# Dealing the copies of the turned attention heads to ScalarE and VectorE in another order, in a transformer-like kernel bound by TensorE

## What is computed

```python
q = einsum('btc,hdc->bhtd', x, Wq); k = einsum('btc,hdc->bhtd', x, Wk)      # 16 heads of 64
w, sel = top_k(einsum('btc,hec->bthe', x, Ws), 2)                          # 2 of 8 experts
v = einsum('bthe,bted->bhtd', mix(sigmoid(w), sel), einsum('btc,edc->bted', x, Wv))
probs = softmax(einsum('bhid,bhjd->bhij', q * scale, k))
attn = einsum('bhij,bhjd->bihd', probs, v)
out = einsum('bthe,bthd,efd->btf', mask_of_top_2(x, Wd), attn, Wo)
x = x + 0.5 * out
```

## Time and profile before

| what | us |
|---|---|
| median of 3 runs (lowest, highest) | 2604.54 (2603.84, 2607.11) |
| the profiled execution, its own time | 2602.62 |
| its span in the trace | 2600.8 |
| busy: PE, DVE, ACT, POOL | 2476.2, 2108.7, 1924.7, 1139.0 |
| busy as a share of the span | 95%, 81%, 74%, 44% |
| clock granted to TensorE, mean | 0.994 of full speed |

### The profile page before, as it was taken

The page is one execution under the profiler, slowest core; times in us unless marked ns, Lnnn a source line. Parts: engine busy times, 40 slices in busy tenths (PEclk is TensorE's granted clock), DMA queues, the critical chain, the costliest instruction groups (busy, mean ns, idle before and its releaser), DMA issues.

```text
span 2600.8 us, 111020 instructions
## 1 busy us (share of the span) xinstructions
PE 2476.2 (95%) x45824; PEld 2319.8 (89%) x45824; DVE 2108.7 (81%) x3498; ACT 1924.7 (74%) x6117; POOL 1139.0 (44%) x1126
## 2 busy tenths in 40 slices
PE   4999999999999999999999999999999999999997
PEld 3899999999899999999999899999999999999987
DVE  4788888888888888888888888888888888888874
ACT  3777777777777777777777777777777777777774
POOL 2344544434434444445345344444444453444431
PEclk8999999999999999999999999999999999999999
DMA  4555555565555655555655555556556556556553
GB/s 128 146 144 153 141 154 144 151 152 155 146 154 149 160 145 153 156 146 152 156 149 152 149 155 150 152 148 162 145 153 156 148 150 158 146 146 159 153 148 97
DMA packets 519346, 387.53 MB, mean 149 GB/s; under 512 B 214080, under 2 KB 436160, under 8 KB 510656
## 3 DMA queue, kind: packets, MB, share of 16 engines
q1 hardware_dynamic: 518416, 379.60, 54.6%
q10 hardware_dynamic: 432, 0.85, 0.1%
HBM read 191.64 MB, written 188.74 MB: 146 GB/s over the span
## 4 chain that ended last, share of the span: by engine, by line
PE 68%; ACT 15%; DVE 8%; issue 7%; POOL 1%; DMA 1%; SPq 0%; ACTq 0%; DVEq 0%; POOLq 0%
PE psT L451 14%; PE psS L408 14%; ACT PB L761 9%; PE psS L490 5%; PE psT L490 5%; PE psT L468 5%; PE psT L421 5%; PE psT L463 5%; PE psT L469 4%; PE psT L470 4%; DVE NMAX L639 4%; PE psT L435 4%; ACT PT L857 3%; ACT QK L770 1%; DVE QK L696 1%
## 5 line engine op out<-in xcount | busy, mean ns | idle before, releaser
L761 ACT ACTIVATE PB<-psS,NMAX 128x256 f32<-128x256 f32 x2048 | 951.4, 489 | 533.4 <-DVE NMAX L639 533.4
L639 DVE TENSOR_REDUCE NMAX<-psS 128x4 f32<-128x1024 f32 x512 | 602.1, 1217 | 79.8 <-PE psS L408 78.8
L451 PE MATMUL psT<-V,PT 128*64 128x64 f32 x16384 | 543.1, 224 | 18.1 <-issue 17.5
L451 PEld LDWEIGHTS psT<-V,PT 128*64 128x64 f32 x16384 | 503.3, 138 | 47.8 <-issue 22.7
L696 DVE TENSOR_TENSOR QK<-psT,QK 128x512 fp32r<-128x512 f32 x512 | 340.9, 688 | 177.0 <-ACT QK L770 174.9
L408 PE MATMUL psS<-QK 64*128 64x256 f32 x6144 | 434.9, 286 | 50.7 <-ACT PT L857 40.4
L408 PEld LDWEIGHTS psS<-QK 64*128 64x128 f32 x6144 | 389.8, 186 | 103.1 <-issue 100.6
L761 ACT ACTIVATION_READ_ACCUMULATOR PB<-psS,NMAX 128x1 f32 x2048 | 454.5, 222 | 0.0
L875 POOL TENSOR_TENSOR BT<-MT,diagv 128x1024 f32<-128x1024 f32 x128 | 307.8, 2405 | 115.3 <-DMA MT<-MIXd 115.3
L770 ACT ACTIVATE QK<-psT 128x512 fp32r<-128x512 f32 x512 | 295.6, 618 | 64.5 <-PE psT L470 49.5
L857 ACT ACTIVATE PT<-psS 128x512 f32<-128x512 f32 x512 | 286.4, 635 | 2.1 <-PE psS L490 1.9
(11 more groups left out here) (119 smaller groups left out, 4572.9 us busy)
## 6 DMA issues: line engine op xcount, KB each, us to landing
Vd<-VM SPq DMA_DIRECT2D x128, 512.0 KB, 3.7
V<-Vd SPq DMA_DIRECT2D x128, 512.0 KB, 5.3
AOd<-AO SPq DMA_DIRECT2D x256, 256.0 KB, 3.6
PJd<-PJ SPq DMA_DIRECT2D x64, 512.0 KB, 2.6
PR<-PJd SPq DMA_DIRECT2D x64, 512.0 KB, 4.1
MIXd<-MIX SPq DMA_DIRECT2D x64, 128.0 KB, 2.5
MT<-MIXd SPq DMA_DIRECT2D x64, 128.0 KB, 4.4
MASKd<-MASKR SPq DMA_DIRECT2D x64, 128.0 KB, 3.3
```

The costliest lines, as they stand in the source:

```text
L451: last = eng.matmul(M[64 * u:64 * u + 64, (t * NT + it) * DH:(t * NT + it + 1) * DH], PT[:, t, jt, cols], V[:, pm % 2, 4 * r + t, jt, :], ...
L639: eng.tensor_reduce(NMAX[:, ab, :, :], psS[:, ab, :, :, :], AX_X, ALU.max, negate=True).then_inc(s_max)
L761: eng.activation(PB[:, ab, j, it, :], psS[:, ab, j, it, :], ACT.Exp, bias=NMAX[:, ab, j, it:it + 1], accum_out=SUM[:, p % 2, it, 4 * r + t ...
```

## The change

DVE takes the copy of head 1 in place of head 3; ACT takes the copy of head 3 in place of head 1. DVE's copy stands ahead of L600 and L604 in quarters 0 and 2 (L600 moves down to just before L604) and where L740 was, at the end, in quarters 1 and 3. ACT's copy of head 0 stands directly behind the last exponentials in quarters 0 and 3, ahead of L828, L834, L846 and L852; in quarters 1 and 2 it stays where it was. Each engine keeps its number of copies.

```diff
2244.36 1.70 PE L408 MATMUL psS<-QK 64*128 64x256 f32 x24 vector_program
+            def copy_second(n):
+                wait_turned(eng, n, 1)
+                wait_full(eng, "product", n - 1)
+                eng.tensor_copy(PT[:, 1].rearrange("p n t -> p (n t)"), turned(n, 1)).then_inc(was_copied(n, 1))
+
             for n in QUARTERS:
...
                         eng.tensor_tensor(QK[:, 1, ab], bank("qk", m).rearrange("p (k t) -> p k t", k=2), QK[:, 0, ab].bitcast(F32), ALU.subtract).then_inc(freed("qk", m))
-                if r == 2 and runs(q):
-                    equal(1, GM[:, :, :], at + 7)
-                if r == 0 and runs(q):
-                    equal(0, GS[:, :, :], at + 1)
                 if r == 1 and runs(q):
...
                     eng.tensor_tensor(xs, bank("attn_w", p - 4)[:, 0:NT * C], xs, ALU.add).then_inc(freed("attn_w", p - 4))
+                if r in (0, 2) and works(n):
+                    copy_second(n)
                 if r == 0 and runs(q):
+                    equal(0, GS[:, :, :], at + 1)
                     weigh(at + 2)
                 if r == 2 and runs(q):
+                    equal(1, GM[:, :, :], at + 7)
                     weigh(at + 8)
...
-                if works(n):
-                    for t in (3,):
-                        wait_turned(eng, n, t)
-                        wait_full(eng, "product", n - 1)
-                        eng.tensor_copy(PT[:, t].rearrange("p n t -> p (n t)"), turned(n, t)).then_inc(was_copied(n, t))
+                if r in (1, 3) and works(n):
+                    copy_second(n)
2244.36 1.70 PE L408 MATMUL psS<-QK 64*128 64x256 f32 x24 scalar_program
+            def copy_turned(n, t):
+                wait_turned(eng, n, t)
+                wait_full(eng, "product", n - 1)
+                eng.activation(PT[:, t].rearrange("p n t -> p (n t)"), turned(n, t), ACT.Copy).then_inc(was_copied(n, t))
...
                 if r in (0, 3):
                     if works(n):
                         exponentials(n, 1, (0,))
                     if works(n + 1):
                         rounded(n)
                     if works(n):
                         exponentials(n, 1, (1,))
+                        copy_turned(n, 0)
...
                 if works(n):
-                    for t in (0, 1, 2):
-                        wait_turned(eng, n, t)
-                        wait_full(eng, "product", n - 1)
-                        eng.activation(PT[:, t].rearrange("p n t -> p (n t)"), turned(n, t), ACT.Copy).then_inc(was_copied(n, t))
+                    if r in (1, 2):
+                        copy_turned(n, 0)
+                    copy_turned(n, 2)
+                    copy_turned(n, 3)
```

## The result

The changed kernel takes 2744.65 us (median of 4 runs, 2735.25 to 2753.71), the kernel before 2605.82 us beside it: 1.0531 times as long, 95% interval 1.0490 to 1.0571. The forecast was 2725 (2640 to 2760), slower. The profiled execution took 2748.70 us with a span of 2746.9 us, so 146.1 us of span are to be accounted for.

A forecast was written before the change was run, and what follows sets the result against it. TensorE, busy 95%, was taken as the bound. To 2602.6 us came -40 + 51 + 15 + 13.5 + 9 = +48.5 and 72 for the port, 2723; with 1.9 us up to the runs' median, 2725 (2640 to 2760).

The forecast's parts named there:

- The gain of 40 us: Quarters 0 and 3: the scores no longer wait for ACT's copies of the turned heads, at most 40 us less.
- Quarter 1, the place of the copy behind L703: A1 and B1: the scores wait for DVE's copy behind the held L703, +1.0 and +0.6 us each, 51 us.
- Quarter 2: DVE's copy behind the second L696 ends after the scores' present start, +0.23 us in 64 quarters, 15 us.
- The bank waits: Turns wait for banks that ACT frees later: B0 +0.52 us each, 13.5 us; C0 and C3 together 9 us.
- The second layer: The port DVE and POOL share: DVE operations held in B0, A0, C0 and D0, 18 + 9 + 36 + 9 = 72 us.
- only the first layer: Rival: POOL doesn't get between L600 and L604, or MT lands later, so NMAX is in time; 2653 us, chance 0.22.
- Faster: Rival: in quarter 1 L881 starts after L703, the 51 us fall to 3; 2596 to 2599 us, chance 0.06.
- Worse: Rival: late NMAX in A1 isn't made good at the quarter's end and waits stack up; 2800 us, chance 0.08.

The follow-up runs named there:

- e1: The changed kernel with the old dealing in quarter 1 alone (ACT copies heads 0, 1, 2, DVE head 3): 2632.62 us, ratio 1.0095.
- e10: The kernel before, ACT's copies 0 and 1 directly behind the exponentials in A0, D0, B3, and POOL's L875 waiting for L604: 2553.95 us.
- e2: The changed kernel with POOL's spread L883 of quarter 1 waiting until DVE has done L604 of quarter 0: 2640.82 us, ratio 1.0126.
- e5: The changed kernel with POOL's L883 waiting for L604, and DVE's copy of head 1 ahead of L704 in quarter 1: 2612.45 us, ratio 1.0021.
- e3: The changed kernel with 16 extra transposes of the identity on TensorE ahead of the scores of A2: 2717.52 us, ratio 1.0433.

## Why the prediction was right, and where it wasn't

- **The gain of 40 us** is there: behind A0 and behind B3 the scores no longer wait. In B3 it is 10 us larger than forecast (-1.30 against -0.9). The 40.4 us were split a little wrong: the 26 waits behind B3 come to 26.0 us, 1.0 each and not 0.9, and the 0.13 us of B0 is in no count of that view. The rest of B3's gain is the waits put down to "issue", 8.6 us less in B3. That those shrink because TensorE waits elsewhere is not shown; in e1 to e10 they lie between 4.1 and 17.6 us over all quarters.
- **Quarter 1, the place of the copy behind L703 (51 us).** With the port's holds of quarter 0 taken away (e2) A1 is 10.69 and B1 10.72 us; with the copy also ahead (e5) they are 9.57 and 10.00. That is 1.1 and 0.7 us, where +1.0 and +0.6 stood.
- **Quarter 2 (15 us):** B2 +0.30 for +0.23.
- **The bank waits (13.5 and 9 us).** B0 without holds is 9.28 us in e2, +0.31 from 8.97, where 0.39 was in the sum (0.52 less the 0.13 of wait it replaces). C0 is +0.93, and the same in e2, without the port's holds. In C3 turn 3 waits for `gates` as foreseen, but for 0.3 us, in 5 of 6, and the mean moves by only +0.03.
- **The second layer (72 us), the port.** In the changed kernel 11 of the B0 have L717 or L720 held for over 1 us, where I counted 14, and the waits that they make are the 1.4 us of the B1 above: these B0 take 10.8 us against 9.28. In the other 15 L600 is held (2.2 to 2.8 us), and B1 is 11.6 us against 10.7. L604 is held as forecast in 24 of the 26 A0, where I counted 21, in pass 30 with its end at 1328.11, 3.0 us behind the scores of A1 (forecast 3.0, 1257.2 against 1254.18). The rule of the Trainium skill (page "SBUF — State Buffer", section "SBUF: two separate sides"), that one side has the pair for the whole instruction, agrees with these rows. It held for L600 too, whose maximum went from 693 to 2842 ns.
- **What was missing: the clock.** The sum let a wait cost its own length; what a wait does to the clock was put at nothing, without a reason. Behind waits of 2.2 us in 18 of the A2 and of 1.4 us in 4 of the B1 the granted clock went to its lower level, and TensorE's busy time grew by 47.7 us. By the lengths of these quarters (11.3 and 10.7 us where the clock stayed up) that is 34 us in A2 and 6 in B1. It is the largest single miss, and most of A2's +1.45 us for +0.23. e3 shows it, as it gives 26 us back by filling the wait in A2.
- **How the sum came out near even so.** Without those 40 us the terms would have been some 15 us too high in all: 10 us more of gain in B3, 4 less of loss in B0, and 8 too much for C and D stand against 6 too little in A1 and 3 in the rest of B1. So 2725 against 2745 is a sum whose mechanisms are mostly borne out and which lacked one, and that it came within 20 us is in part luck, as the errors have opposite signs.

The rivals: *only the first layer* (2653) is what e2 makes, 2641, and needs the port's holds gone. *Faster* needed L881 later than L703; L889 still runs ahead of L704, 1334.24 against 1335.05. *Worse* by lateness that stacks up didn't happen; A3 is at its 9.71 us again.

## What to carry to other kernels

A copy that releases the bound engine goes to the engine that is free when its input is ready, and ahead of that engine's other work; dealing copies evenly says nothing about that. Look at what the copy now stands behind, and whether that can be held by a neighbour: here each move of DVE's operations past one another decided whether they met a 2.4 us operation of GpSimd, and one wait on GpSimd's side, on work with slack, took that away for good. And a wait of TensorE is to be priced with what may follow it: where the clock falls, the work behind it is slow too, here in 18 of 24 waits of 2.2 us.

## What the runs showed of the hardware

- TensorE's granted clock fell behind 18 of 24 single idle stretches of 2.2 us in A2 (in pass 30 to a mean of 0.60 over the next 4.3 us) and behind 4 of 11 of 1.1 to 1.6 us ahead of B1 (pass 31: 0.68 over 5.3 us), in a kernel that was otherwise busy over 90%. In the kernel before, stretches of up to 1.4 us left its mean at 1.00 over 100 to 2500 us. A filler of 1.91 us in the same stretch kept the 24 scores at 1.70 us.
- The same kernel isn't slowed alike each time: the mean granted clock of the changed kernel's four runs was 0.975, 0.977, 0.984 and 0.982, at 2748.7, 2753.7, 2740.6 and 2735.3 us. e2's four runs, at 0.994 to 0.997, lie within 5 us.
- A DVE operation with two SBUF operands that came 1.0 us ahead of the first spread's end was served between POOL's two back-to-back spreads (L703, 1.58 us); one that came as the second began was held until both were done (L706 in e5, 2.52 us).
- DVE's copies out of PSUM were never held by POOL: L635 has a mean of 684 ns over 256, and none is over 693.
- TensorE's waits put down to "issue" ahead of the product end 2.2 to 3.0 us after the start of a DMA packet of the kind "instruction", in 24 of 24 places in the kernel before.
